# The scale of a state-space layer's gates taken on GpSimd: one power of minus one half in place of a root on ScalarE and a reciprocal on VectorE

## The chip, the cores and the metric

The kernel runs on one core of a Trainium2 chip. A core has five engines that each take their own instructions in order and meet only at semaphores: TensorE (PE, matmuls), VectorE (DVE), ScalarE (ACT), GpSimd (POOL) and SyncE (SP, which issues DMAs). The metric is the device time of one execution in microseconds.

## The reference

A block of three residual layers for 4 sequences of 128 tokens with 128 channels: a cross attention with 16 heads over 2048 keys, a gated linear recurrence (a state-space layer), and a two-layer perceptron with binary weights. The change lies in the second. Cut to it:

```python
u_scaled = exp(log_gamma) * einsum('btd,nd->btn', u, Win_n)
delta_raw, b_raw, c_raw = split(einsum('btd,kd->btk', u, Wp) + bp, 3)
delta = softplus(delta_raw + delta_bias)
a = minimum(exp(-delta * softplus(alpha_log)), 1.0 - 1e-4)
b, c = tanh(b_raw), tanh(c_raw)
p, r, q = a * a + c * c, b * b, a * b
disc = (p - r) * (p - r) + 4.0 * q * q
lam_max = 0.5 * (p + r + sqrt(disc + EPS))
scale = maximum(sqrt(lam_max + EPS), 1.0)
a, b, c = a / scale, b / scale, c / scale
# state z_t = a_t z_{t-1} + b_t u_scaled_t, by a scan over t
y = einsum('btn,on->bto', c * z_shifted, Wout_n)
```

## The kernel before

The attention comes first and takes most of the span: a loop over 128 units (4 sequences x 8 pairs of heads x 4 chunks of 512 keys). Behind it the rest of the block works on all 512 tokens, in two halves of 256 columns (`cols(h)`, two sequences each); channels lie on the 128 partitions. A half of a gate is a tile of 128x256 in fp32. All gates are named slices of one buffer, which the profile shows as `k_parts` since they reuse its memory; `q_r` in the profile is `q_r1`, and `q` is the tile of the scan's states (`STATE`).

Each engine's program is written out by hand, and its order is the order in which it works. For the gates it is:

- ScalarE does absolute value, exp, ln, tanh, squares and the root of the discriminant `G_D` (L1010, semaphore `disc_root`). Then it takes the root of `0.5 * G_L + EPS` for each half (L1013, `scale_ready`), touches Gelu so that its table is loaded (L1015), and goes on with the copies and the Gelus of the perceptron (L1021).
- VectorE adds `G_S + G_D` into `G_L` for both halves (L1488), clamps it from below at 2.0 (L1490, `lam_ready`), and multiplies U by the gain and B (`scale_input`, L1485). Then, for half 0: `invert(0)`, the reciprocal of `G_L` (L1504, `inv_ready`); `scale_gates(0)`, A and U times `G_INV` (L1509, L1511); `scan(0)` (L1518); `outputs(0)`, C times the state (L1499). Then `invert(1)`; the sum of y of half 0 with its layer norm's moments (L1521 to L1426); `scale_gates(1)`; the normalisation of half 0 (L1432); `scan(1)`; `outputs(1)`; and the same norm for half 1.
- GpSimd waits for `inv_ready` and multiplies C by `G_INV` for each half (L1164), and then takes the power of minus one half of the layer norm's variances (`root_inv_halves(1)`, L1035), two columns for each half. The exponent is the tile `neg_half`, filled with -0.5.
- TensorE projects the raw gates (L750 to L758), waits for `scale_ready` of half 0, and multiplies a tile of ones by itself 11 times (L352, fillers whose result nobody reads; the profile counts two matmuls for each). Then come y of half 0 (L733), 12 more fillers, the transposes of half 0 (L358), y of half 1, the hidden layer (L773) and the output layer (L782), the last two for half 0 and half 1 in turn.
- VectorE adds the result to the residual (L1541), and SyncE stores it.

Of the kernel before, what the change touches and what calls it, by code (L numbers as in the profile page):

```python
# [28 lines left out]
ALU = mybir.AluOpType  # L29
ACT = mybir.ActivationFunctionType  # L30
AX = mybir.AxisListType

P = 128
# [5 lines left out]
EPS = 1e-12  # L39
# [4 lines left out]
def perceiver_block(nc, x, ctx_in, mask, Wq, bq, Wk, bk, Wv, bv, Wo, bo, W_in, W_out, Wp, bp,  # L44
# [34 lines left out]
    with ctx:  # L79
        def sb(name, shape, dt=F32):  # L80
            return ctx.enter_context(nc.sbuf_tensor(name, shape, dt))
# [32 lines left out]
        neg_half = sb("neg_half", [P, B])  # L114
# [35 lines left out]
        sv = sb("sv", [P, 12])  # L150
# [57 lines left out]
        def once(name):  # L208
            return sems[name] if name in sems else sem(name)
# [6 lines left out]
        HALF = TOK // 2  # L216
# [8 lines left out]
        def cols(h):  # L225
            return slice(HALF * h, HALF * h + HALF)
# [120 lines left out]
        def _(pe):  # L347
# [389 lines left out]
            def finish():  # L737
                pe.wait_ge(o_ready, B)
                for h in range(2):
                    turn_half(h, o_nat, once("oN_turned"))  # L740
                for h in range(2):
                    pe.wait_ge(once("oNT_ready"), h + 1)
                    by_token(h, PROJ, xnT, wT[:, W_O, :], once("attn_done"))
                keep_busy(TURN, WARM_LN2)
                for h in range(2):
                    pe.wait_ge(once("ln_ready"), 2 * h + 2)
                    turn_half(h, xn, once("ln_turned"))
                for h in range(2):
                    pe.wait_ge(once("lnT_ready"), h + 1)
                    pe.matmul(bank(h, RAW_DELTA)[:, 0:HALF], wT[:, W_P, :], xnT[:, cols(h)], start=True, stop=True  # L750
                              ).then_inc(once("ssm_done"), 1)
                for h in range(2):
                    for i in range(2):
                        t = pe.matmul(bank(h, RAW_BC)[:, HALF * i:HALF * i + HALF], wT[:, W_P + 1 + i, :],
                                      xnT[:, cols(h)], start=True, stop=True)
                    t.then_inc(once("ssm_done"), 1)
                for h in range(2):
                    pe.matmul(bank(h, RAW_U)[:, 0:HALF], wT[:, W_IN, :], xnT[:, cols(h)], start=True, stop=True  # L758
                              ).then_inc(once("ssm_done"), 1)
                pe.wait_ge(once("scale_ready"), 1)  # L760
                keep_busy(TURN, WARM_Y)
                def project_y(h):
                    pe.wait_ge(once("yhat_ready"), h + 1)
                    by_token(h, Y, q_r1, wT[:, W_OUT, :], once("y_done"))

                def turn_mlp(h):
                    pe.wait_ge(once("ln_ready"), B + 2 * h + 2)
                    turn_half(h, xn, once("ln_turned"))

                def hidden(h):  # L770
                    pe.wait_ge(once("lnT_ready"), 2 + h + 1)
                    for i in range(HB):
                        t = pe.matmul(bank(h, HIDDEN + i // 2)[:, HALF * (i % 2):HALF * (i % 2) + HALF], w1T[:, i, :],  # L773
                                      xnT[:, cols(h)], start=True, stop=True)
                        if i % 2 == 1:
                            t.then_inc(once("h_done"), 1)

                def mlp_out(h, blocks):
                    for i in blocks:
                        pe.wait_ge(once("gelu_ready"), HB * h + i + 1)  # L780
                        for b in halves[h]:
                            t = pe.matmul(bank(h, OUT)[:, P * (b % 2):P * (b % 2) + P],  # L782
                                          probs[:, i, 0, P * b:P * b + P], w2T[:, i, :],
                                          start=(i == 0 and b % 2 == 0), stop=(i == HB - 1), skip_group_check=True)
                    return t

                project_y(0)
                keep_busy(4 + TURN, WARM_Y0)
                turn_mlp(0)
                project_y(1)  # L790
                hidden(0)
                mlp_out(0, range(0, 2))
                turn_mlp(1)
                mlp_out(0, range(2, HB)).then_inc(once("mlp_done"), 1)
                hidden(1)
                mlp_out(1, range(HB)).then_inc(once("mlp_done"), 1)
# [13 lines left out]
        def _(act):  # L810
# [197 lines left out]
            for h in range(2):  # L1008
                act.wait_ge(once("disc_ready"), h + 1)
                act.activation(G_D[:, cols(h)], G_D[:, cols(h)], ACT.Sqrt).then_inc(once("disc_root"), 1)  # L1010
            for h in range(2):
                act.wait_ge(once("lam_ready"), h + 1)
                act.activation(G_L[:, cols(h)], G_L[:, cols(h)], ACT.Sqrt, bias=sv[:, 9:10], scale=0.5  # L1013
                               ).then_inc(once("scale_ready"), 1)
            act.activation(sv[:, 8:9], ones[:, 0:1], ACT.Gelu)  # L1015
            for h in range(2):
                act.wait_ge(once("ln_turned"), 2 + h + 1)
# [8 lines left out]
        def _(gp):  # L1026
# [133 lines left out]
            root_inv_halves(0)  # L1160

            for h in range(2):
                gp.wait_ge(once("inv_ready"), h + 1)
                gp.tensor_tensor(G_CS[:, cols(h)], G_C[:, cols(h)], G_INV[:, cols(h)], ALU.mult  # L1164
                                 ).then_inc(once("c_scaled"), 1)
# [4 lines left out]
        def _(dve):  # L1170
# [268 lines left out]
            def each(s, op, *waits):  # L1439
                before_this = own_steps[0]  # L1440
                for h in range(2):
                    for name in waits:
                        if name == "own":
                            dve.wait_ge(once("own_step"), before_this - 1 + h)
                        else:
                            dve.wait_ge(once(name), h + 1)
                    op(h, cols(h)).then_inc(once("own_step" if s == "own" else s), 1)
                    if s == "own":
                        own_steps[0] += 1
# [33 lines left out]
            def scale_input(h):  # L1483
# [1 line left out]
                dve.scalar_tensor_tensor(U_S[:, cols(h)], bank(h, RAW_U)[:, 0:HALF], sv[:, 7:8], G_B[:, cols(h)],  # L1485
                                         ALU.mult, ALU.mult).then_inc(once("u_ready"), 1)

            each("own", lambda h, t: dve.tensor_tensor(G_L[:, t], G_S[:, t], G_D[:, t], ALU.add),  # L1488
                 "s_ready", "disc_root")
            each("lam_ready", lambda h, t: dve.tensor_scalar(G_L[:, t], G_L[:, t], 2.0, None, ALU.max), "own")  # L1490
            for h in range(2):
                scale_input(h)
            by_t = lambda a, h: a[:, cols(h)].rearrange("p (b t) -> p b t", t=T)
# [1 line left out]
            def outputs(h):  # L1495
# [2 lines left out]
                dve.wait_ge(once("first_step_ready"), 1)  # L1498
                dve.tensor_tensor(by_t(q_r1, h)[:, :, 1:T], by_t(G_CS, h)[:, :, 1:T], by_t(STATE, h)[:, :, 0:T - 1],  # L1499
                                  ALU.mult).then_inc(once("yhat_ready"), 1)  # L1500

            def invert(h):
                dve.wait_ge(once("scale_ready"), h + 1)
                dve.reciprocal(G_INV[:, cols(h)], G_L[:, cols(h)]).then_inc(once("inv_ready"), 1)  # L1504

            def scale_gates(h):
                t = cols(h)
# [5 lines left out]
            def scan(h):  # L1513
                dve.wait_ge(once("a_scaled"), h + 1)
                dve.wait_ge(once("u_scaled"), h + 1)
                for b in halves[h]:
# [3 lines left out]

            add_y = lambda h: dve.scalar_tensor_tensor(by_half(x_sb, h), bank(h, Y)[:, 0:HALF], norm_inv[:, 1:2],  # L1521
                                                       by_half(x_sb, h), ALU.mult, ALU.add)
            invert(0)
            scale_gates(0)
            scan(0)
            outputs(0)
            invert(1)
            add_and_moments(1, 0, add_y, "y_done")
            scale_gates(1)
            normalise_half(1, 0)  # L1530
# [50 lines left out]
```

## Time and profile before

| | |
|---|---|
| median of 3 runs | 290.27 us (286.96 to 290.95) |
| profiled execution | 289.0 us |
| its span, first to last instruction | 287.2 us |
| mean granted clock of TensorE | 0.97 of full |
| busy: TensorE, VectorE, ScalarE, GpSimd | 259.2, 223.5, 209.8, 100.8 us |
| instructions | 9806 |

All rows come from the one profiled execution. Its own time is 1.8 us above its span (launch and end). It lies 1.3 us under the median of the three runs.

### The profile page before, as it was taken

The page shows a single profiled execution, that of the slowest core. Times are in us where ns is not written, and L with a number is a line of the kernel's source. Part 1 is how long each engine was busy: PE and PEld are TensorE (multiplying, and loading weights), DVE is VectorE, ACT ScalarE, POOL GpSimd, SP SyncE. Part 2 cuts the span into 40 slices and gives each one's busy share as a digit, 9 for nine tenths or more (in the row PEclk, how much of TensorE's full clock was granted, in tenths as well). Part 3 has the DMA queues.
Part 4 walks back from the last instruction along what each step waited for, and adds up shares of the span by engine and source line. Part 5 has one row for each costly group of instructions (what it writes and reads, how often), then busy time and mean ns, then how long its engine had stood idle before and what let it go on. Part 6 is the DMA issues. An engine that isn't in the chain of part 4 may idle for free.

```text
span 287.2 us, 9806 instructions
## 1 busy us (share of the span) xinstructions
PE 259.2 (90%) x3981; PEld 187.0 (65%) x3981; DVE 223.5 (78%) x407; ACT 209.8 (73%) x441; POOL 100.8 (35%) x225
## 2 busy tenths in 40 slices
PE   7898689999999999999999999999999996750975
PEld 6485357676766676676777777777777664640955
DVE  5776888887877998878888888979888960529971
ACT  2675358888888878888888888888888787198232
POOL 6366775633344343333334454511111220100220
PEclk9999979999999999999999999999999999795799
DMA  6896944786432323242424332222222100000001
GB/s 200 294 316 174 286 120 140 229 235 192 159 123 80 119 68 121 66 129 79 135 74 135 93 105 66 67 67 66 66 88 76 34 3 5 1 0 0 0 0 41
DMA packets 21081, 30.55 MB, mean 106 GB/s; under 512 B 4272, under 2 KB 15052, under 8 KB 20908
## 3 DMA queue, kind: packets, MB, share of 16 engines
q1 hardware_dynamic: 17708, 28.00, 32.0%
q0 software_dynamic: 624, 1.06, 1.4%
q10 hardware_dynamic: 2704, 0.85, 1.3%
q8 instruction: 33, 0.54, 0.8%
q14 instruction: 12, 0.10, 0.1%
HBM read 22.43 MB, written 7.47 MB: 104 GB/s over the span
## 4 chain that ended last, share of the span: by engine, by line
PE 75%; DVE 10%; DMA 5%; ACT 4%; issue 4%; POOL 1%; ACTq 1%; SPq 0%; POOLq 0%; DVEq 0%
PE ps L504 24%; PE ps L487 14%; PE ps L463 11%; PE ps L597 5%; PE ps L515 4%; PE ps L358 4%; PE ps L558 4%; PE ps L550 4%; DMA w_kv<-in_L_xattn_Wq_dram 2%; DVE pmax L1315 2%; DMA k_rows<-k_parts_dram 1%; DMA k_parts_dram<-k_parts 1%; ACT probs L887 1%; DVE k_parts L1504 1%; PE ps L374 1%
## 5 line engine op out<-in xcount | busy, mean ns | idle before, releaser
L1315 DVE TENSOR_REDUCE pmax<-ps 128x2 f32<-128x1024 f32 x128 | 156.1, 1224 | 28.6 <-PE ps L463 27.9
L887 ACT ACTIVATE probs<-ps 128x512 f32<-128x512 f32 x256 | 138.8, 596 | 18.8 <-PE ps L487 16.5
L504 PE MATMUL ps<-probs,v_all 128*9 128x128 f32 x2048 | 80.5, 275 | 1.6 <-ACT probs L887 1.0
L463 PE MATMUL ps<-k_rows,q_all 56*128 56x512 bf16 x256 | 77.9, 384 | 3.0 <-DVE pmax L1315 2.2
L487 PE MATMUL ps<-q_max,k_rows 59*128 59x128 bf16 x1024 | 80.1, 218 | 0.2 <-DVE q_max L1327 0.2
L487 PEld LDWEIGHTS ps<-q_max,k_rows 59*128 59x128 bf16 x1024 | 54.3, 94 | 4.1 <-ACT probs L887 2.2
L504 PEld LDWEIGHTS ps<-probs,v_all 128*9 128x9 f32 x2048 | 43.3, 90 | 15.9 <-ACT probs L887 1.9
L1124 POOL CAST max_cols<-negmax 128x2 bf16<-128x2 f32 x32 | 6.1, 192 | 120.0 <-DVE negmax L1321 120.0
L463 PEld LDWEIGHTS ps<-k_rows,q_all 56*128 56x128 bf16 x256 | 23.2, 93 | 21.9 <-issue 11.3
L352 PE MATMUL ps<-ones 128*128 128x128 f32 x76 | 12.7, 338 | 11.0 <-ACT k_parts L1013 10.1
L352 PEld LDWEIGHTS ps<-ones 128*128 128x128 f32 x76 | 12.1, 252 | 11.4 <-ACT k_parts L1013 10.5
L820 ACT ACTIVATE v_all<-ps 128x256 f32<-128x256 f32 (+1 forms) x24 | 10.9, 456 | 9.0 <-PE ps L374 5.0
L597 PE MATMUL ps<-power 128*128 128x128 f32 x96 | 17.1, 300 | 0.0
L597 PEld LDWEIGHTS ps<-power 128*128 128x128 f32 x96 | 12.5, 190 | 5.2 <-issue 3.9
L515 PEld LDWEIGHTS ps<-gather,oT_sb 128*128 128x128 f32 x64 | 9.5, 188 | 7.6 <-issue 7.3
L1072 POOL TENSOR_TENSOR k_r<-k,k_parts 128x512 f32<-128x512 f32 x12 | 14.1, 1174 | 1.0
L1078 POOL TENSOR_TENSOR k_parts<-k_r,k_parts 128x512 bf16<-128x512 f32 x12 | 13.9, 1162 | 1.0
L820 ACT ACTIVATE ctxT<-ps 128x512 f32<-128x512 f32 x16 | 9.5, 595 | 6.1 <-PE ps L358 6.0
L515 PE MATMUL ps<-gather,oT_sb 128*128 128x18 f32 x64 | 12.7, 274 | 0.5 <-ACT oT_sb L820 0.5
L820 ACT ACTIVATE xnT<-ps 128x256 f32<-128x256 f32 (+2 forms) x6 | 2.3, 383 | 14.0 <-PE ps L358 14.0
L550 PE MATMUL ps<-ctxT,kvT 128*128 128x256 f32 x32 | 11.2, 431 | 1.2 <-DVE q_max L1327 1.2
L358 PE MATMUL ps<-ident,ctx_buf 128*128 128x128 f32 x64 | 11.0, 299 | 1.0 <-DMA ctx_buf<-in_ctx_dram 1.0
(186 smaller groups left out, 329.3 us busy)
## 6 DMA issues: line engine op xcount, KB each, us to landing
k_rows<-k_parts_dram SPq DMA_DIRECT2D x59, 192.0 KB
k_parts_dram<-k_parts SPq DMA_DIRECT2D x16, 384.0 KB, 3.9
ctx_buf<-in_ctx_dram SPq DMA_DIRECT2D x16, 256.0 KB, 6.1
k_rows<-k_parts_dram SPq DMA_DIRECT2D x59, 32.0 KB
mask_sb<-in_mask_1x1xSxS_ff_dram SPq DMA_DIRECT2D x1, 1024.0 KB, 8.6
q_all<-q_rows_dram SPq DMA_DIRECT2D x2, 336.0 KB
k_rows<-k_parts_dram POOLq DMA_DIRECT2D x3, 192.0 KB, 4.0
q_rows_dram<-q_parts SPq DMA_DIRECT2D x2, 288.0 KB, 3.9
```

Of the source, the lines that this page charges most:

```text
L352: pe.matmul(ps[:, bank, 0:P], ones[:, :], ones[:, :], start=True, stop=True)
L358: return pe.transpose(dst, src, ident[:, :])
L463: return pe.matmul(ps[:, bank + h, :], q_all[rows, i % PAIRS, i // PAIRS, :], k_rows[rows, i % 4, 512 * c:512 * c + 512], start=not masked ...
L487: t = pe.matmul(dst, k_rows[rows, i % 4, at:at + P], q_max[rows, i % 2, :], start=not masked, stop=True, skip_group_check=masked)
L504: t = pe.matmul(ps[at:at + HEAD_COLS, 6, 0:P], v_all[:, KT * (i // PAIRS) + 4 * c + j, first + HEAD_COLS * h: first + HEAD_COLS * h + HEAD ...
L515: return pe.matmul(ps[:, 7, 384:384 + 2 * HEAD_COLS], oT_sb[:, i % 2, :], gather[:, :], start=True, stop=True)
L550: pe.matmul(ps[:, 7, half], kvT[:, 0, :], ctxT[:, n % EARLY, half], start=True, stop=True).then_inc(k_done, 1)
L597: t = pe.matmul(ps[:, 7, P * w:P * w + P], power[:, k % 2, w, :], power[:, k % 2, w, :], start=True, stop=True)
L820: act.activation(dst, src, ACT.Copy).then_inc(s, n)
L887: act.activation(probs[:, u % CHUNKS, h, :], ps[:, key_bank(u, h), :], ACT.Exp).then_inc(probs_ready, 1)
L1072: gp.tensor_tensor(r1, k_all, k_parts[:, 0, keys], ALU.subtract).then_inc(split_k_step, 1)
L1315: dve.tensor_reduce(pmax[:, i % 2, :, c], ps[:, bank:bank + 2, :], AX.X, ALU.max).then_inc(pmax_ready, 1)
```

## The change

ScalarE's second pair of roots and VectorE's pair of reciprocals are gone. The sum on VectorE takes 2 EPS with it, and the clamp multiplies by 0.5, so that `G_L` now holds the square of the scale. GpSimd raises that tile of 128x256 to the power -0.5, one half of the tokens at a time, ahead of its multiplication of C; the exponent is one column of `neg_half` read for all 256. TensorE's fillers wait for both clamps in place of the first root.

```diff
--- before.py
+++ after.py
@@ -757,7 +757,7 @@
                 for h in range(2):
                     pe.matmul(bank(h, RAW_U)[:, 0:HALF], wT[:, W_IN, :], xnT[:, cols(h)], start=True, stop=True
                               ).then_inc(once("ssm_done"), 1)
-                pe.wait_ge(once("scale_ready"), 1)
+                pe.wait_ge(once("lam_ready"), 2)
                 keep_busy(TURN, WARM_Y)
                 def project_y(h):
                     pe.wait_ge(once("yhat_ready"), h + 1)
@@ -1008,10 +1008,6 @@
             for h in range(2):
                 act.wait_ge(once("disc_ready"), h + 1)
                 act.activation(G_D[:, cols(h)], G_D[:, cols(h)], ACT.Sqrt).then_inc(once("disc_root"), 1)
-            for h in range(2):
-                act.wait_ge(once("lam_ready"), h + 1)
-                act.activation(G_L[:, cols(h)], G_L[:, cols(h)], ACT.Sqrt, bias=sv[:, 9:10], scale=0.5
-                               ).then_inc(once("scale_ready"), 1)
             act.activation(sv[:, 8:9], ones[:, 0:1], ACT.Gelu)
             for h in range(2):
                 act.wait_ge(once("ln_turned"), 2 + h + 1)
@@ -1160,6 +1156,9 @@
             root_inv_halves(0)
 
             for h in range(2):
+                gp.wait_ge(once("lam_ready"), h + 1)
+                gp.tensor_tensor(G_INV[:, cols(h)], G_L[:, cols(h)], neg_half[:, 0:1].broadcast_to((P, HALF)), ALU.pow
+                                 ).then_inc(once("inv_ready"), 1)
                 gp.wait_ge(once("inv_ready"), h + 1)
                 gp.tensor_tensor(G_CS[:, cols(h)], G_C[:, cols(h)], G_INV[:, cols(h)], ALU.mult
                                  ).then_inc(once("c_scaled"), 1)
@@ -1485,9 +1484,9 @@
                 dve.scalar_tensor_tensor(U_S[:, cols(h)], bank(h, RAW_U)[:, 0:HALF], sv[:, 7:8], G_B[:, cols(h)],
                                          ALU.mult, ALU.mult).then_inc(once("u_ready"), 1)
 
-            each("own", lambda h, t: dve.tensor_tensor(G_L[:, t], G_S[:, t], G_D[:, t], ALU.add),
+            each("own", lambda h, t: dve.scalar_tensor_tensor(G_L[:, t], G_D[:, t], 2.0 * EPS, G_S[:, t], ALU.add, ALU.add),
                  "s_ready", "disc_root")
-            each("lam_ready", lambda h, t: dve.tensor_scalar(G_L[:, t], G_L[:, t], 2.0, None, ALU.max), "own")
+            each("lam_ready", lambda h, t: dve.tensor_scalar(G_L[:, t], G_L[:, t], 2.0, 0.5, ALU.max, ALU.mult), "own")
             for h in range(2):
                 scale_input(h)
             by_t = lambda a, h: a[:, cols(h)].rearrange("p (b t) -> p b t", t=T)
@@ -1498,10 +1497,6 @@
                 dve.wait_ge(once("first_step_ready"), 1)
                 dve.tensor_tensor(by_t(q_r1, h)[:, :, 1:T], by_t(G_CS, h)[:, :, 1:T], by_t(STATE, h)[:, :, 0:T - 1],
                                   ALU.mult).then_inc(once("yhat_ready"), 1)
-
-            def invert(h):
-                dve.wait_ge(once("scale_ready"), h + 1)
-                dve.reciprocal(G_INV[:, cols(h)], G_L[:, cols(h)]).then_inc(once("inv_ready"), 1)
 
             def scale_gates(h):
                 t = cols(h)
@@ -1520,11 +1515,9 @@
 
             add_y = lambda h: dve.scalar_tensor_tensor(by_half(x_sb, h), bank(h, Y)[:, 0:HALF], norm_inv[:, 1:2],
                                                        by_half(x_sb, h), ALU.mult, ALU.add)
-            invert(0)
             scale_gates(0)
             scan(0)
             outputs(0)
-            invert(1)
             add_and_moments(1, 0, add_y, "y_done")
             scale_gates(1)
             normalise_half(1, 0)
```

## Rows read from the trace of the kernel before

**Rows 1.** The page: busy shares, and the chain that ended last

```profile
PE 259.2 (90%) x3981; PEld 187.0 (65%) x3981; DVE 223.5 (78%) x407; ACT 209.8 (73%) x441; POOL 100.8 (35%) x225
...
PE 75%; DVE 10%; DMA 5%; ACT 4%; issue 4%; POOL 1%; ACTq 1%; SPq 0%; POOLq 0%; DVEq 0%
...
PE ps L504 24%; PE ps L487 14%; PE ps L463 11%; PE ps L597 5%; PE ps L515 4%; PE ps L358 4%; PE ps L558 4%; PE ps L550 4%; DMA w_kv<-in_L_xattn_Wq_dram 2%; DVE pmax L1315 2%; DMA k_rows<-k_parts_dram 1%; DMA k_parts_dram<-k_parts 1%; ACT probs L887 1%; DVE k_parts L1504 1%; PE ps L374 1%
```

**Rows 2.** The chain that ended last, 265 to 288 us: start, duration, what

```profile
265.77 1.67 DVE k_parts L1504
...
270.06 1.66 DVE k_parts L1504
```

**Rows 3.** Timeline, 264 to 285 us: start, duration, instruction, [idle before]

```profile
264.50 0.48 DVE L1490 TENSOR_SCALAR k_parts<-k_parts 128x256 f32<-128x256 f32 x2
...
264.82 0.91 ACT L1013 ACTIVATE k_parts<-k_parts,sv 128x256 f32<-128x256 f32 x2 [1.10 <-DVE k_parts L1490]
...
265.38 4.22 PE L352 MATMUL ps<-ones 128*128 128x128 f32 x22 [10.05 <-ACT k_parts L1013]
...
267.47 0.43 DVE L1509 TENSOR_TENSOR k_parts<-k_parts 128x256 f32<-128x256 f32 x1
...
267.51 0.97 POOL L1164 TENSOR_TENSOR k_parts<-k_parts 128x256 f32<-128x256 f32 x1 [17.08 <-DVE k_parts L1504]
...
267.81 0.95 DVE L1511 TENSOR_TENSOR k_parts<-k_parts 128x256 f32<-128x256 f32 x1
...
271.80 0.73 POOL L1164 TENSOR_TENSOR k_parts<-k_parts 128x256 f32<-128x256 f32 x1 [3.32 <-DVE k_parts L1504]
...
272.87 0.17 DVE L1426 TENSOR_SCALAR var_eps<-mv 128x2 f32<-128x2 f32 x1
...
273.11 0.80 POOL L1035 TENSOR_TENSOR rstd<-var_eps,neg_half 128x2 f32<-128x2 f32 x1 [0.58 <-DVE var_eps L1426]
...
273.95 0.60 DVE L1432 TENSOR_SCALAR xn<-x_sb,mv,rstd 128x128 f32<-128x128 f32 x2 [0.26 <-POOL rstd L1035]
...
274.61 0.44 PE L358 MATMUL ps<-ident,xn 128*128 128x128 f32 x2 [1.10 <-DVE xn L1432]
...
277.33 1.70 ACT L1021 ACTIVATE probs<-ps,vec 128x256 f32<-128x256 f32 x4 [1.86 <-PE ps L773]
...
278.03 0.69 POOL L1035 TENSOR_TENSOR rstd<-var_eps,neg_half 128x2 f32<-128x2 f32 x1 [4.12 <-DVE var_eps L1426]
...
282.32 1.95 PE L782 MATMUL ps<-w2T,probs 128*128 128x128 f32 x16
```

**Rows 4.** GpSimd's instructions grouped by line and shape: busy, mean ns, idle

```profile
L1126 POOL TENSOR_TENSOR nm_r<-negmax,max_cols 128x2 f32<-128x2 f32 x32 | 6.3, 196 | 2.6
...
L1035 POOL TENSOR_TENSOR rstd<-var_eps,neg_half 128x2 f32<-128x2 f32 x4 | 2.9, 729 | 17.5 <-DVE var_eps L1426 17.5
...
L1156 POOL TENSOR_TENSOR x_bo<-x_sb,bo_rows 128x128 f32<-128x128 f32 x4 | 1.8, 454 | 0.0
...
L1164 POOL TENSOR_TENSOR k_parts<-k_parts 128x256 f32<-128x256 f32 x2 | 1.7, 849 | 20.4 <-DVE k_parts L1504 20.4
...
L1052 POOL TENSOR_TENSOR rstd<-var_eps,neg_half 128x3 f32<-128x3 f32 x1 | 0.9, 877 | 0.6 <-DVE var_eps L1181 0.6
...
L1159 POOL TENSOR_TENSOR norm_inv<-norm_inv,neg_half 128x2 f32<-128x2 f32 x1 | 0.7, 714 | 0.0
...
L1048 POOL TENSOR_TENSOR rstd<-var_eps,neg_half 128x1 f32<-128x1 f32 x1 | 0.6, 563 | 2.8 <-DVE var_eps L1181 2.8
```

**Rows 5.** TensorE by stretch: length, busy (matmuls), granted clock, DMA share, GB/s

```profile
258.00:260.00 2.00, 0.00 (x0) 0.58 0.00 0
...
266.00:268.00 2.00, 2.00 (x11) 0.50 0.00 0
...
268.00:270.00 2.00, 1.60 (x12) 0.86 0.00 0
...
274.60:284.30 9.70, 8.62 (x56) 1.00 0.05 15
```

## Prediction

> **What bounds the kernel now.** I read the page first: TensorE is busy 90% of the span and holds 75% of the chain that ended last, but GpSimd only 35% [rows 1]. Those shares describe the attention loop, whose three matmul lines (L504, L487, L463) alone are 49% of the chain. The change lies in the gates after it, so I read the timeline of that stretch. Up to about 274 us it is a chain of small steps on VectorE and ScalarE, and TensorE only turns filler matmuls. The three steps to look at are the two reciprocals of 128x256, which stand on VectorE and on the chain with 1.67 and 1.66 us [rows 2], and the root ahead of them on ScalarE, 0.91 us for two halves, of which the first lies between the clamp and the first reciprocal [rows 3]. GpSimd is idle for 17.08 us before its first multiply there [rows 3]. The idleness is real; what the new work costs on that engine is the question, and the view that groups GpSimd's instructions by shape answers it.
>
> **What the power costs.** The kernel already takes powers of minus one half on GpSimd, on tiny tiles: 563 ns for one column of 128 partitions (x1), 714 ns and a mean of 729 ns for two (x1 and x4), 877 ns for three (x1) [rows 4]. The step from one to two columns is 151 ns, from two to three 163 ns, and from one to three 314/2 = 157 ns each. That is a price by the column, above a fixed 563 - 157 = 406 ns. The ordinary operations are in the same view for scale: a subtraction takes 196 ns for two columns, an addition 454 ns for 128, a multiplication 849 ns on average for 256 [rows 4]; from 2 to 128 columns that is (454 - 196)/126 = 2.0 ns a column, and from there to 256 3.1 ns or, by the undisturbed one of 0.73 us [rows 3], 2.1 ns. So an ordinary operation's price by the column is the same for short and for long rows, and the power's is some 75 times as high. The change asks for 256 columns, twice. By the line through the three sizes one costs 0.41 + 256 x 0.157 = 40.6 us.
>
> No row shows a power of more than three columns, so I bound it. Below stands the ordinary operation on the same tile, 0.73 us [rows 3]. Above, the steepest pair of single readings, 563 ns and the 0.80 us of one two-column power [rows 3, 4], gives 237 ns a column and 61 us. I take 40.6 us, since the three sizes lie on one line within 6 ns a column and the ordinary operations show that such a line holds on this engine; the shallowest pair, 563 ns and the 0.69 us of another two-column power [rows 3, 4], gives 0.127 us a column and some 33 us. The exponent is now one column read 256 times in place of a tile of its own; I cost that at nothing, since 256 exponents had to be delivered either way.
>
> Two rules of the Trainium skill speak the other way. The page GPSIMD Engine Reference, section 3.1 (Elementwise: side-by-side cycle accounting), gives some 2.6 cycles an element for a two-input operation; read as a rule for all of them, an estimate by it is 0.56 us and a fixed part for this tile. The trace agrees for the multiplication and not for the power. Its section 7 (Performance pitfalls for Q7 kernels) says that a dependent chain of fp32 steps goes faster when unrolled into at least four independent ones. No row here shows whether the power's code does so for long rows.
>
> **Part by part.** The addition on VectorE becomes one with a second addend, and the clamp gets a multiplication by 0.5. I leave the additions as they are and the clamps of both halves at 0.48 us from 264.50 on [rows 3], with a few hundredths for an error. Cost nothing: it is the same number of passes over the same tile. The first root waited for the first clamp and began at 264.82 [rows 3]; less 0.04 us for the handover the clamp ends at 264.78.
>
> Removed from ScalarE: the two roots, 0.91 us [rows 3]. Behind them is only the load of the table for the activation of the hidden layer, which comes up to 0.9 us earlier and is not needed before the first such activation at 277.33 [rows 3]. Removed from VectorE: the two reciprocals [rows 2].
>
> Added on GpSimd: two powers, each ahead of the multiplication that it already did. The engine takes its instructions in order, so the queue is power 0, C x INV of half 0, power 1, C x INV of half 1, and then the two-column power for the layer norm of half 0. What is queued there behind power 1 is needed by VectorE for that normalisation; and VectorE itself waits in order at the scaling of A of half 0, with the scan, the outputs, the sum of y and all of the second half queued behind it. The scaling of U needs INV as well, so nothing of the scan can begin.
>
> The new sequence, with a wait of 0.07 us for each handover (the variance ends at 272.87 + 0.17 = 273.04, and the power that waits for it begins at 273.11 [rows 3]):
> - power 0 begins at 264.78 + 0.07 = 264.85 and ends at 305.45;
> - C x INV of half 0, with the longer of its two durations, 0.97 us [rows 3]: 305.45 + 0.07 + 0.97 = 306.49;
> - power 1 has waited for nothing (both clamps are long done): it ends at 306.49 + 40.6 = 347.09;
> - C x INV of half 1: 348.13; the layer norm's power of 0.80 us: 348.93; VectorE's normalisation begins 0.04 us later, at 348.97.
> Before, that normalisation began at 273.95 [rows 3]. From it on the order of work is the old one, to the end. The scalings of half 1 run on VectorE from 347.14 and, with the first half's 0.43 and 0.95 us [rows 3], end at 348.5 and stay hidden. First half: gates at 305.5, y at about 308 (the outputs were ready at 270.06, when the second reciprocal began, 2.6 us after the first ended [rows 2]); all of its work fits under power 1, with over 30 us to spare. The shift is 348.97 - 273.95 = 75.0 us. With C for one power it is 2C - 6.2 us; the 6.2 is what was between clamp and normalisation before and is not done any more or is overlapped.
>
> **TensorE's clock.** The wait that starts the eleven filler matmuls moves from the first root to the second clamp, so the 4.22 us of them (from 265.38 today) begin some 0.3 us earlier and end near 269, almost 40 us before y of half 0 [rows 3]. The granted clock falls in a stretch without matmuls, to a mean of 0.58 in 258 to 260, and is 0.50 (1.2 GHz) while the fillers begin. They ran at 0.50 in 266 to 268, and the mean of 0.86 in 268 to 270 puts the return to full (2.4 GHz) at 268.6, 3.2 us after the first of them [rows 5]. Today the tail is all at 2.4 GHz: 1.00 in 274.6 to 284.3 [rows 5]. After the change the matmuls of y of half 0 and the fillers behind it are hidden under power 1, and then TensorE has nothing until 349 us. The tail starts at 1.2 GHz. Its matmuls are nearly one chain, from the transposes at 274.61 to the last line's 1.95 us from 282.32 [rows 3]: TensorE is busy for 8.6 of those 9.7 us [rows 5]. If some 3 to 4 us of it run at half speed before the clock is back, they do 1.5 to 2 us less work: I add 2.0 us. The bounds are nothing (the fillers' clock survives) and 8.6 us (it never rises in the tail).
>
> **The sum.** 75.0 + 2.0 = +77.0 us. The profiled execution took 289.0 us, 287.2 of them the span; the span would be 364.2 and the time 366.0. The median of the three runs, 290.27, is 1.3 us above the profiled one and they spread over 4 us; on the median it is 367.3, and I say 367.
>
> **Rivals.**
> 1. The power overlaps its columns once there are many of them, as it can't with three. At a quarter of 157 ns a column C = 0.41 + 10.0 = 10.4 us, the shift 2 x 10.4 - 6.2 = 14.6, with the clock 16.6: 307 us. For it: only sizes 1 to 3 are seen. (The section 7 of the Trainium skill's page above describes such a gain.) Against it: neither two nor three columns are cheaper than a line. Chance 0.12.
> 2. The power costs what an ordinary operation on the tile does, C = 0.73, and what the small ones show is a fixed cost that grows for another reason. (It is what section 3.1 of that page of the Trainium skill would have.) Then INV of half 0 is there at 265.6 and VectorE goes on when its multiplication of U by the gain and B is done and the reciprocal would begin, at 265.77, in place of 265.77 + 1.67 = 267.44 [rows 2]: 1.7 us won; the second reciprocal (1.66 us on the chain) covered the way of y through TensorE, 0.9 us of which stays as a wait, so 0.8 more. 2.5 us faster, 288 us. By 2C - 6.2 + 2.0 the change wins as long as C stays under 2.1 us, 7 ns a column. Against it: two columns alone take 0.7 us where an ordinary one takes 0.2. Chance 0.03.
> 3. The line, but the clock stays at 1.2 GHz through the tail: 367 + 6.6 = 374 us. Against it: the fillers brought it up in some 3 us. Chance 0.09.
> 4. Dearer than the line, 61 us each: 2 x 61 - 6.2 + 2 = +118, 408 us, should long rows or other values (before, the power saw variances; now numbers from one upwards) cost more. Chance 0.04.
>
> **How the numbers follow.** Forecast 0.72, rivals 0.12, 0.03, 0.09 and 0.04. What a measurement of this kernel can tell from no change is about 2%, 5.8 us. No case reaches 5.8 us of gain, since the best is 2.5; I leave 0.01. Within 2% needs 2C - 6.2 + 2.0 < 5.8, C under 5.0 us or 18 ns a column: rival 2 and the cheap end of rival 1, 0.04 in all. Slower: 0.95. The range: by the line 151 to 163 ns a column are 364 to 370 us; the shallowest pair is 352; rival 3 reaches 374, and a little on both sides for the spread of the runs: 345 to 380, which leaves out rivals 1, 2 and 4, 0.19.
>
> **What would show it.** Right: two powers on GpSimd of about 40 us each, GpSimd's busy time at some 180 us, VectorE waiting for them twice, for almost 40 and then for some 36 us; a granted clock of 0.50 at the start of the tail; C x INV still under 1 us. The attention loop before 244 us is the same. Wrong: powers of 10 us or less; or the second half's power overlapped by something that I hold to be queued behind it.

## The result, and the profile after

The changed kernel takes 366.81 us (median of 4 runs, 365.78 to 367.89) against 290.03 us (4 runs): 1.267 times as long, 95% interval 1.257 to 1.277. The forecast was 367. Here and below, ratios and their intervals leave out executions in a slower state that some runs show, so they differ slightly from the quotient of the medians. The profiled execution has a span of 364.9 us, 77.7 more than before.

The page of the changed kernel, with its busy times, the granted clock in 40 slices and the chain by engine, answers to [rows 1]:

```profile
PE 263.0 (72%) x3981; PEld 190.3 (52%) x3981; DVE 220.9 (61%) x405; ACT 209.1 (57%) x439; POOL 183.8 (50%) x227
...
PEclk9999899999999999999999999989665555855559
...
PE 63%; POOL 24%; DVE 6%; ACT 3%; issue 2%; DMA 1%; ACTq 0%; DVEq 0%; POOLq 0%
```

TensorE's busy time is the same to within 4 us, VectorE and ScalarE have a little less, and GpSimd has 83 us more, which it did not have on the chain before and now has: 24% of the chain against 1%. The clock row shows where the time lies, in the last quarter of the span, with TensorE at half clock for most of it. The first 244 us hold the same 233.3 us of matmuls in both kernels.

The timeline of the changed kernel from the clamp to the last addition answers to [rows 3] (lines have moved: the clamp is L1489, the power L1160, C x INV L1163, the scalings L1504 and L1506, the layer norm's power L1031, the normalisation L1431):

```profile
264.36 0.49 DVE L1489 TENSOR_SCALAR k_parts<-k_parts 128x256 f32<-128x256 f32 x2
...
264.73 41.13 POOL L1160 TENSOR_TENSOR k_parts<-k_parts,neg_half 128x256 f32<-128x256 f32 x1 [14.44 <-DVE k_parts L1489]
...
305.89 0.43 DVE L1504 TENSOR_TENSOR k_parts<-k_parts 128x256 f32<-128x256 f32 x1 [40.25 <-POOL k_parts L1160]
...
306.23 0.95 DVE L1506 TENSOR_TENSOR k_parts<-k_parts 128x256 f32<-128x256 f32 x1
...
306.86 41.29 POOL L1160 TENSOR_TENSOR k_parts<-k_parts,neg_half 128x256 f32<-128x256 f32 x1
...
348.19 0.43 DVE L1504 TENSOR_TENSOR k_parts<-k_parts 128x256 f32<-128x256 f32 x1 [36.68 <-POOL k_parts L1160]
...
349.16 0.87 POOL L1031 TENSOR_TENSOR rstd<-var_eps,neg_half 128x2 f32<-128x2 f32 x1
...
350.07 0.60 DVE L1431 TENSOR_SCALAR xn<-x_sb,mv,rstd 128x128 f32<-128x128 f32 x2 [0.59 <-POOL rstd L1031]
...
352.85 3.62 PE L773 MATMUL ps<-xnT,w1T 128*128 128x256 f32 x8
...
362.14 0.42 DVE L1534 TENSOR_TENSOR xn<-ps,x_bo 128x256 f32<-128x256 f32 x1 [2.99 <-PE ps L782]
```

Read it as one queue. The power of half 0 begins 0.08 us after its clamp, which ends at 264.65, and lasts 41.13 us; VectorE has been idle for 40.25 us when its first scaling begins, just after the power's end. Half 0's scalings, scan, y and the moments of its layer norm are done under the second power, 41.29 us, after which VectorE has been idle for 36.68 us. From the clamp's start to the normalisation's start it is 350.07 - 264.36 = 85.7 us; before it was 273.95 - 264.50 = 9.45 [rows 3]. That is 76.3 us of the 77.7. The rest is behind it: from the normalisation to the last addition 362.14 - 350.07 = 12.07 us. In the kernel before the same addition began at 284.31, so that it was 10.36: 1.7 us more.

TensorE's windows in that tail answer to [rows 5] (length, busy time with its number of matmuls, granted clock, DMA share, GB/s):

```profile
350.00:352.00 2.00, 0.85 (x3) 0.50 0.00 0
...
352.00:354.00 2.00, 2.00 (x7) 0.50 0.00 0
...
354.00:356.00 2.00, 2.00 (x6) 0.50 0.00 0
...
356.00:358.00 2.00, 2.00 (x17) 0.85 0.00 0
```

The tail begins at 0.50 (1.2 GHz) and the clock is back during 356 to 358. The hidden layer of half 0 takes 3.62 us at the low clock; that of half 1, at the high one, 1.89. Eight executions with a power in them and TensorE idle for over 6 us ahead of the tail were profiled; from the normalisation to the last addition they took 11.71 to 12.51 us.

### The profile page after: what moved, and what is told of

It reads as the page before. It is cut to its first block, busy times and chain, and to the rows that moved or that the text cites. A ratio compares the mean times of both kernels' runs of the same rounds, so it can differ in the third digit from the quotient of the medians.

```text
span 364.9 us, 9804 instructions
## 1 busy us (share of the span) xinstructions
PE 263.0 (72%) x3981; PEld 190.3 (52%) x3981; DVE 220.9 (61%) x405; ACT 209.1 (57%) x439; POOL 183.8 (50%) x227
## 4 chain that ended last, share of the span: by engine, by line
PE 63%; POOL 24%; DVE 6%; ACT 3%; issue 2%; DMA 1%; ACTq 0%; DVEq 0%; POOLq 0%
POOL k_parts L1160 23%; PE ps L504 19%; PE ps L487 11%; PE ps L463 9%; PE ps L597 4%; PE ps L358 3%; PE ps L515 3%; PE ps L558 3%; PE ps L550 3%; PE ps L374 2%; PE ps L369 2%; PE ps L773 1%; DMA x_sb<-in_x_dram 1%; DVE pmax L1314 1%; PE ps L782 1%
## 5 line engine op out<-in xcount | busy, mean ns | idle before, releaser
L1160 POOL TENSOR_TENSOR k_parts<-k_parts,neg_half 128x256 f32<-128x256 f32 x2 | 82.4, 41211 | 14.4 <-DVE k_parts L1489 14.4
L1504 DVE TENSOR_TENSOR k_parts<-k_parts 128x256 f32<-128x256 f32 x2 | 0.9, 426 | 76.9 <-POOL k_parts L1160 76.9
L358 PE MATMUL ps<-ident,xn 128*128 128x128 f32 x16 | 3.9, 346 | 39.4 <-DVE xn L1431 38.2
L733 PE MATMUL ps<-wT,q_r 128*128 128x128 f32 x8 | 2.4, 461 | 40.2 <-DVE q_r L1498 40.2
L358 PEld LDWEIGHTS ps<-ident,xn 128*128 128x128 f32 x16 | 2.2, 168 | 40.3 <-DVE xn L1431 38.8
L733 PEld LDWEIGHTS ps<-wT,q_r 128*128 128x128 f32 x8 | 1.9, 321 | 40.8 <-DVE q_r L1498 40.8
L352 PE MATMUL ps<-ones 128*128 128x128 f32 x76 | 13.5, 353 | 10.7 <-DVE k_parts L1489 9.7
L352 PEld LDWEIGHTS ps<-ones 128*128 128x128 f32 x76 | 13.0, 268 | 11.1 <-DVE k_parts L1489 10.1
```

The costliest lines, as they stand in the source:

```text
L352: pe.matmul(ps[:, bank, 0:P], ones[:, :], ones[:, :], start=True, stop=True)
L358: return pe.transpose(dst, src, ident[:, :])
L1160: gp.tensor_tensor(G_INV[:, cols(h)], G_L[:, cols(h)], neg_half[:, 0:1].broadcast_to((P, HALF)), ALU.pow).then_inc(once("inv_ready"), 1)
```

## Experiments

**Is it a price by the column? (e1)** Each power is cut into pieces; nothing else changes.

```diff
-gp.tensor_tensor(G_INV[:, cols(h)], G_L[:, cols(h)], neg_half[:, 0:1].broadcast_to((P, HALF)), ALU.pow
-                 ).then_inc(once("inv_ready"), 1)
+at = HALF * h
+for n in ((16, 48, 64, 128), (4, 8, 32, 84, 128))[h]:
+    ...
+    gp.tensor_tensor(G_INV[:, at:at + n], G_L[:, at:at + n], neg_half[:, 0:1].broadcast_to((P, n)), ALU.pow
+                     ).then_inc(once("inv_ready" if last else "piece"), 1)
+    at += n
```

> Each power is cut into pieces of 16, 48, 64 and 128 columns (half 0) and of 4, 8, 32, 84 and 128 (half 1), the same columns in all. Price by the column (my theory): a piece of n columns takes 0.41 + 0.159 n us, so 1.0, 1.7, 5.5, 8.0, 10.6, 13.8 and 20.8 us for 4, 8, 32, 48, 64, 84 and 128 columns, and the kernel is some 3 us longer than the changed one for the seven added fixed parts, 370 us. Rival (short rows cost more by the column than long ones): the line bends between 3 columns and 256, and the sum of the pieces is well above 85 us.

370.11 us, one run. The groups of GpSimd by shape, in this kernel (busy, mean ns of one, idle before):

```profile
L1165 POOL TENSOR_TENSOR k_parts<-k_parts,neg_half 128x128 f32<-128x128 f32 x2 | 41.4, 20720 | 0.2
...
L1165 POOL TENSOR_TENSOR k_parts<-k_parts,neg_half 128x64 f32<-128x64 f32 x1 | 10.5, 10512 | 0.0
...
L1165 POOL TENSOR_TENSOR k_parts<-k_parts,neg_half 128x32 f32<-128x32 f32 x1 | 5.4, 5407 | 0.0
...
L1165 POOL TENSOR_TENSOR k_parts<-k_parts,neg_half 128x16 f32<-128x16 f32 x1 | 2.9, 2893 | 14.5 <-DVE k_parts L1495 14.5
...
L1165 POOL TENSOR_TENSOR k_parts<-k_parts,neg_half 128x8 f32<-128x8 f32 x1 | 1.6, 1627 | 0.0
...
L1165 POOL TENSOR_TENSOR k_parts<-k_parts,neg_half 128x4 f32<-128x4 f32 x1 | 1.2, 1184 | 0.0
```

The pieces of 48 and 84 columns took 7.99 and 13.73 us. From 8 to 16 columns it is 158 ns a column, from 16 to 128 (20720 - 2893)/112 = 159, and from 128 to the changed kernel's 256, 41.2 us on average, 160. The line does not bend. Only the piece of 4 columns is off it, with 1.18 us where the line has 1.04. The pieces of half 0 span 42.14 us and those of half 1 42.66, 84.8 together and not well above 85, so the rival is out.

**Does the kernel lose anything but the powers' own time? (e2)** The operation of the two instructions becomes a multiplication, so that the scale is not computed; the rest is the changed kernel.

```diff
-neg_half[:, 0:1].broadcast_to((P, HALF)), ALU.pow
+neg_half[:, 0:1].broadcast_to((P, HALF)), ALU.mult
```

> The operation of the two big instructions on GpSimd is a multiplication in place of the power, so the scale is wrong and the rest of the work the same; everything else is as in the changed kernel. My theory (all of the loss is the power's price by the column): 0.73 to 0.97 us for each, 2.5 us faster than the kernel before, 287.5 us, and the tail at full clock. Rival (GpSimd in this place costs more than its own time, by handovers and by instructions that run in order behind it): slower than the kernel before, by 1 us or more.

287.43 us (10 runs) against 289.39 for the kernel before beside it (13 runs), a ratio of 0.9955, interval 0.9915 to 0.9996. So the powers are all of the loss. With a multiplication in their place (the output is then wrong) the kernel takes what the kernel before takes or slightly less: the difference is under 1% and barely clear of the noise. Its timeline:

```profile
262.76 0.50 DVE L1489 TENSOR_SCALAR k_parts<-k_parts 128x256 f32<-128x256 f32 x2
...
263.13 0.61 POOL L1160 TENSOR_TENSOR k_parts<-k_parts,neg_half 128x256 f32<-128x256 f32 x1 [14.44 <-DVE k_parts L1489]
...
263.31 5.07 PE L352 MATMUL ps<-ones 128*128 128x128 f32 x22 [9.72 <-DVE k_parts L1489]
...
266.80 0.42 DVE L1498 TENSOR_TENSOR q_r<-k_parts,q 128x254 f32<-128x254 f32 x1
...
268.17 1.06 PE L733 MATMUL ps<-wT,q_r 128*128 128x128 f32 x4
...
269.27 0.48 DVE L1516 SCALAR_TENSOR_TENSOR x_sb<-ps,norm_inv,x_sb 128x256 f32<-128x256 f32 x1 [2.04 <-PE ps L733]
...
282.03 0.42 DVE L1534 TENSOR_TENSOR xn<-ps,x_bo 128x256 f32<-128x256 f32 x1 [2.99 <-PE ps L782]
```

From the clamp to the last addition it is 282.03 - 262.76 = 19.27 us against 284.31 - 264.50 = 19.81 before: 0.5 us won inside the stretch, where I had said 2.5. (The clamp also began 1.7 us earlier, at 262.76, which is no gain of the change: the first transpose behind the attention began between 243.0 and 246.3 us in the executions profiled here.) The outputs of half 0 end at 267.22, but y begins at 268.17 behind the fillers, which start after 9.72 us without a matmul, at half clock, and take 5.07 us. VectorE then waits 2.04 us for y, as its row shows. How long the fillers hold y differs between executions: the same 22 matmuls took 4.11 us in the changed kernel's profile, 4.46 in f1's and 5.07 here.

**Fewer fillers in its way (g3).** The same with 8 fillers ahead of y of half 0 and 15 behind.

```diff
-WARM_LN2, WARM_Y, WARM_Y0 = 8, 11, 12
+WARM_LN2, WARM_Y, WARM_Y0 = 8, 8, 15
```

> e2 (a multiplication in place of the power) with 8 fillers ahead of y of half 0 and 15 behind it, in place of 11 and 12. In e2 y of half 0 stood behind the fillers: they ended at 268.4 while the scan's outputs were there at 267.2, and y ran at half clock. If that is what kept e2's gain from the clamp to the last addition at 0.5 us in place of 2.5: y begins when the outputs are ready and another 0.5 to 1 us is won, 286.8 us. Rival (the gain is lost elsewhere, since the layer norm behind y is itself no faster): no difference from e2.

```profile
263.54 0.48 DVE L1489 TENSOR_SCALAR k_parts<-k_parts 128x256 f32<-128x256 f32 x2
...
267.57 0.42 DVE L1498 TENSOR_TENSOR q_r<-k_parts,q 128x254 f32<-128x254 f32 x1
...
268.05 0.71 PE L733 MATMUL ps<-wT,q_r 128*128 128x128 f32 x4 [0.18 <-DVE q_r L1498]
```

The outputs end at 267.99 and y begins at 268.05. The last addition begins at 281.56, so the stretch is 18.02 us: 1.8 us shorter than before, and 1.2 shorter than with 11 fillers. So between these two traces the fillers were what held back 1.2 of the 2.0 us that were missing. The median does not show it: 287.59 us (12 runs), ratio 0.9956, interval 0.9921 to 0.9992, the same as with 11, where 286.8 was expected. A difference of 1.2 us is within what these runs spread by, and 11 fillers at 4.11 us would have held y for some 0.2 us only (an estimate from e2's row of the outputs, 267.22, and its first filler, 263.31). The step is shown in two traces and not in the time.

**Is it the repeated exponent column? (e3)** The exponents come from a tile of their own.

```diff
+neg_tile = sb("neg_tile", [P, 256])
+gp.memset(neg_tile[:, :], -0.5).then_inc(once("neg_tile_ready"), 1)
...
-neg_half[:, 0:1].broadcast_to((P, HALF)), ALU.pow
+neg_tile[:, :], ALU.pow
```

> The exponents come from a tile of 128x256 filled with -0.5 in place of one column read 256 times. My theory: 41.2 us for a power, as with the one column, 367 us. Rival (the repeated column is what is slow): a power of 20 us or less and a time under 330 us.

366.73 us, one run, and the first of its powers:

```profile
264.86 41.24 POOL L1163 TENSOR_TENSOR k_parts<-k_parts,neg_tile 128x256 f32<-128x256 f32 x1 [14.77 <-DVE k_parts L1492]
```

41.24 us: it is not the column.

**Is it the values? (e4)** Every base is 1.0, so that the scale is lost.

```diff
-dve.tensor_scalar(G_L[:, t], G_L[:, t], 2.0, 0.5, ALU.max, ALU.mult)
+dve.tensor_scalar(G_L[:, t], G_L[:, t], 0.0, 1.0, ALU.mult, ALU.add)
```

> The clamp is replaced by a multiplication by 0 and an addition of 1, so that every base is exactly 1.0 and the scale is lost; the powers are the same in shape. My theory (a fixed number of steps for every column): 41.2 us each, 367 us. Rival (the price depends on the values, for instance by steps repeated until they settle): a power shorter by a quarter or more, 347 us or less.

364.72 us, one run, with

```profile
262.81 41.13 POOL L1160 TENSOR_TENSOR k_parts<-k_parts,neg_half 128x256 f32<-128x256 f32 x1 [14.44 <-DVE k_parts L1489]
...
304.94 41.30 POOL L1160 TENSOR_TENSOR k_parts<-k_parts,neg_half 128x256 f32<-128x256 f32 x1
```

The durations are those of the changed kernel within 0.01 us; the 2 us in the time are the start, 262.81 in place of 264.73. The price does not depend on these values. The clamp keeps every base of the changed kernel at 1.0 or above, so what is compared is such numbers with exactly 1.0; other bases on long rows were not tried.

**By the column or by the element? (f1)** Half 0's power in two instructions of 64 partitions.

```diff
+for k in range(1 if h else 2):
+    rows_ = slice(0, P) if h else slice(64 * k, 64 * k + 64)
...
-    gp.tensor_tensor(G_INV[:, cols(h)], G_L[:, cols(h)], ...
+    gp.tensor_tensor(G_INV[rows_, cols(h)], G_L[rows_, cols(h)], ...
```

> The power of half 0 is taken as two instructions of 64 partitions x 256 columns, one after the other; half 1 as in the changed kernel. My theory (a price by the column, whatever the number of partitions): 41.2 us for each of the two, and the kernel 41 us longer than the changed one, 408 us. Rival (a price by the element, so that 64 partitions cost half): 20.6 us each, 367 us.

409.22 us, one run, and in the groups of GpSimd:

```profile
L1165 POOL TENSOR_TENSOR k_parts<-k_parts,neg_half 64x256 f32<-64x256 f32 x2 | 82.2, 41118 | 14.5 <-DVE k_parts L1494 14.4
...
L1165 POOL TENSOR_TENSOR k_parts<-k_parts,neg_half 128x256 f32<-128x256 f32 x1 | 41.3, 41308 | 0.0
```

64 partitions cost what 128 do. The Trainium skill's page GPSIMD Engine Reference, section 2 (Architecture), says that each of eight cores works on its own 16 partitions, 16 lanes wide. If so, fewer partitions leave lanes idle and save no step, and the trace agrees, with 41.12 and 41.31 us.

**One half alone (f2).** Half 0 by root and reciprocal, half 1 by the power.

```diff
-for h in range(2):
+for h in range(1):
     act.wait_ge(once("lam_ready"), h + 1)
     act.activation(G_L[:, cols(h)], G_L[:, cols(h)], ACT.Sqrt, bias=sv[:, 9:10], scale=0.5
...
 for h in range(2):
+    if h == 1:
+        gp.wait_ge(once("lam_ready"), 2)
+        gp.tensor_tensor(G_INV[:, cols(1)], G_L[:, cols(1)], neg_half[:, 0:1].broadcast_to((P, HALF)), ALU.pow
+                         ).then_inc(once("inv_ready"), 1)
     gp.wait_ge(once("inv_ready"), h + 1)
...
-each("lam_ready", lambda h, t: dve.tensor_scalar(G_L[:, t], G_L[:, t], 2.0, None, ALU.max), "own")
+each("lam_ready", lambda h, t: dve.tensor_scalar(G_L[:, t], G_L[:, t], 2.0, 0.5 if h else None, ALU.max, *((ALU.mult,) if h else ())), "own")
...
-invert(1)
```

> Half 0 has its root and reciprocal as in the kernel before; only half 1 is taken by a power on GpSimd, which stands there behind the multiplication of C of half 0. My theory: GpSimd is free at 268.5, the power ends at 309.7, C x INV and the layer norm's power follow, and VectorE's normalisation begins at 311.6 in place of 273.95: 37.7 us, and 1.7 for the tail at half clock, 329.5 us. Rival (half 0's power, being the first on the path, holds most of the loss, and that of half 1 is partly covered by half 0's work): under 310 us.

328.03 us (4 runs), ratio 1.132, interval 1.126 to 1.139: 38 us longer than the kernel before.

```profile
263.17 0.49 DVE L1494 TENSOR_SCALAR k_parts<-k_parts 128x256 f32<-128x256 f32 x2
...
267.11 41.31 POOL L1165 TENSOR_TENSOR k_parts<-k_parts,neg_half 128x256 f32<-128x256 f32 x1
...
310.33 0.60 DVE L1436 TENSOR_SCALAR xn<-x_sb,mv,rstd 128x128 f32<-128x128 f32 x2 [0.59 <-POOL rstd L1035]
...
322.81 0.42 DVE L1544 TENSOR_TENSOR xn<-ps,x_bo 128x256 f32<-128x256 f32 x1 [2.99 <-PE ps L782]
```

From the clamp to the normalisation it is 47.2 us, 37.7 more than before, as expected; the tail is 12.48. Half 1's power alone costs half of the loss, although half 0's work up to the moments of its layer norm goes on under it, since that work ends under 5 us after the power begins (at 271.68, against 267.11). The rival is out.

**The clock in the tail (f3, g1, g2).** 150 fillers in place of 12 behind y of half 0, then 174, the latter beside the changed kernel once more.

```diff
-WARM_LN2, WARM_Y, WARM_Y0 = 8, 11, 12
+WARM_LN2, WARM_Y, WARM_Y0 = 8, 11, 150
```

> 150 filler matmuls in place of 12 behind y of half 0, so that TensorE works until shortly before the tail begins, under the second power. My theory (the tail's 1.7 us more are the granted clock): the tail runs at 2.4 GHz from its first matmul and the kernel takes 1.7 us less than the changed one, 365.1 us. Rival (the tail is longer for another reason, such as the order in which the two halves arrive): 366.8 us, with the clock up.

367.62 us (4 runs). It did not do what it was for: the fillers end at 344.17, TensorE is idle for 6.39 us, and the tail starts at the low clock again. Windows and one line of the timeline:

```profile
320.00:340.00 20.00, 20.00 (x182) 1.00 0.00 1
...
340.00:350.00 10.00, 4.17 (x38) 0.95 0.00 0
...
350.00:352.00 2.00, 1.03 (x3) 0.50 0.00 0
```

```profile
350.56 0.69 PE L358 MATMUL ps<-ident,xn 128*128 128x128 f32 x2 [6.39 <-DVE xn L1431]
```

> As f3, with 174 fillers in place of 150: at 0.22 us each at full clock they end near 349.5, about 1 us before the tail's first transpose, where 150 left TensorE idle for 6.39 us and the clock back at 0.50. Theory (the tail's additional time is the clock): the tail at 1.00 from its first matmul, 10.4 us from the normalisation's start to the last addition as in the kernel before instead of 12.1, and 1.7 us less than the changed kernel beside it. Rival (the two halves' order or the handovers): 12.1 us at full clock too.

> The changed kernel once more, as the measure for the run beside it: 366.8 us.

366.32 us (8 runs) for 174 fillers, 367.54 us (6 runs) for the changed kernel beside it. The ratios to the kernel before, 1.265 (1.260 to 1.269) and 1.268 (1.262 to 1.274), overlap, so the 1.2 us between them are not settled by the times. The 174's timeline and windows:

```profile
352.63 0.60 DVE L1431 TENSOR_SCALAR xn<-x_sb,mv,rstd 128x128 f32<-128x128 f32 x2 [0.59 <-POOL rstd L1031]
...
353.29 0.44 PE L358 MATMUL ps<-ident,xn 128*128 128x128 f32 x2 [0.97 <-DVE xn L1431]
...
354.39 0.71 PE L733 MATMUL ps<-wT,q_r 128*128 128x128 f32 x4 [0.67 <-DVE q_r L1498]
...
354.94 3.26 PE L773 MATMUL ps<-xnT,w1T 128*128 128x256 f32 x8
...
364.06 0.42 DVE L1534 TENSOR_TENSOR xn<-ps,x_bo 128x256 f32<-128x256 f32 x1 [2.99 <-PE ps L782]
```

```profile
350.00:352.00 2.00, 2.00 (x20) 1.00 0.00 0
...
352.00:354.00 2.00, 0.75 (x5) 1.00 0.00 0
...
354.00:356.00 2.00, 1.61 (x8) 0.83 0.00 0
...
356.00:358.00 2.00, 2.00 (x7) 0.50 0.00 0
```

This tail starts at 1.00, and its transposes and y have the durations of the kernel before, 0.44 and 0.71 us. Then the clock falls to 0.50 in the middle of the hidden layer, which takes 3.26 us, while TensorE is busy 1.61 of 2 us. The tail is 11.43 us, against 12.51 in the changed kernel profiled beside it (351.10 to 363.61), 12.07 in its first profile and 10.36 before. It is 0.3 us under the shortest of the eight tails that start at the low clock, 11.71 (e3). So half of the theory holds: up to the start of the hidden layer, 2.31 us behind the normalisation in both, this tail has the times of the kernel before, and the 1.1 us by which it is longer come with the low clock behind it. But keeping TensorE busy up to the tail did not keep the clock for the tail. Why it fell there stays open.

**A version without GpSimd (f4).** On the kernel before, the inverse as exp(-0.5 ln x) on ScalarE.

```diff
-    act.activation(G_L[:, cols(h)], G_L[:, cols(h)], ACT.Sqrt, bias=sv[:, 9:10], scale=0.5
+    act.activation(G_L[:, cols(h)], G_L[:, cols(h)], ACT.Ln, bias=sv[:, 9:10], scale=0.5
                    ).then_inc(once("scale_ready"), 1)
+for h in range(2):
+    act.wait_ge(once("scale_ready"), h + 1)
+    act.activation(G_INV[:, cols(h)], G_L[:, cols(h)], ACT.Exp, scale=-0.5).then_inc(once("inv_ready"), 1)
...
-invert(0)
...
-invert(1)
```

> On the kernel before: the scale's inverse as exp(-0.5 ln(x)) on ScalarE, with no reciprocal on VectorE and no power on GpSimd. It adds two table loads of 1.28 us. My theory: the load for the logarithm hides beside VectorE's addition and clamp, both logarithms end at 265.8, the load for the exponential at 267.1, and the first half is ready at 267.5, as before (267.44); the second reciprocal is gone from VectorE, of which 0.8 us were not covered: 0.8 us faster, 289.3 us. Rival (the table loads stand on the path with more than that): 1 us slower or more.

288.87 us (12 runs) against 290.03 (17 runs), ratio 0.9958, interval 0.9914 to 1.0003: no difference that the measurement can tell.

```profile
264.58 0.49 DVE L1494 TENSOR_SCALAR k_parts<-k_parts 128x256 f32<-128x256 f32 x2
...
267.77 0.43 DVE L1509 TENSOR_TENSOR k_parts<-k_parts 128x256 f32<-128x256 f32 x1 [1.92 <-ACT k_parts L1017]
...
267.81 1.83 POOL L1168 TENSOR_TENSOR k_parts<-k_parts 128x256 f32<-128x256 f32 x2 [17.31 <-ACT k_parts L1017]
...
269.16 1.08 DVE L1518 TENSOR_TENSOR_SCAN q<-k_parts 128x128 f32<-128x128 f32 x2
...
273.91 0.60 DVE L1436 TENSOR_SCALAR xn<-x_sb,mv,rstd 128x128 f32<-128x128 f32 x2 [0.26 <-POOL rstd L1039]
```

The first half is ready at about 267.7, where 267.5 was expected. From the clamp to the normalisation it is 9.33 us against 9.45 before: 0.1 us of the expected 0.8. Both halves' INV now come close together, so GpSimd does both its multiplications from 267.81 to 269.64, beside VectorE's scaling of U and the scan. The scan takes 1.08 us where it took 0.74 before. Measured from the clamp, the outputs are ready 0.55 us later: 0.2 because the scalings begin later and 0.3 by the scan. So most of what the missing reciprocal gave is gone.

## Why the prediction was right, step by step

**The power's price.** Forecast 40.6 us, from three tiles of 1 to 3 columns; measured 41.13 and 41.29. The slope was 157 ns a column by [rows 4] and is 159 to 160 on long rows. The two together are 82.4 us against 81.2: the 1.2 us missing from the sum are here. That the step to long rows was sound is shown by e1, that the exponent's form costs at most 0.1 us by e3, and that setting every base to 1.0 changes nothing by e4. The Trainium skill's page GPSIMD Engine Reference says in section 7 (Performance pitfalls for Q7 kernels) that a dependent chain of fp32 steps goes faster when unrolled into at least four; how the power's code is built no run shows, but no such gain appears in it, 159 ns a column up to 128 columns and 160 beyond. The same page of the Trainium skill gives 2.6 cycles an element for two inputs in section 3.1 (Elementwise: side-by-side cycle accounting), by the prediction's estimate 0.56 us and a fixed part for this tile. The multiplication in the power's place is near that, 0.61 and 0.79 us in e2; the measured power is 68 times the 0.61. Rivals 1 and 4 fell with the two durations of 41 us, and e1 shows why for rival 1: long rows are no cheaper by the column.

**The order on GpSimd and VectorE.** Forecast: power 0, multiplication, power 1, multiplication, layer norm's power, then the normalisation, 84.12 us from the start of power 0 (264.85 to 348.97). Measured 85.34 (264.73 to 350.07), and the difference is the powers' 1.2. VectorE waited 40.25 and 36.68 us, forecast almost 40 and some 36. f2 confirms that the two powers add up with no cover.

**The tail.** Forecast +2.0 us for the low clock, measured +1.7 in the profiled execution and 2.1 in that of the changed kernel's second profile (12.51 against 10.36). That the size came out is in part luck. The prediction had 3 to 4 us at the low clock; the mean of 0.85 in 356 to 358 puts the return at 356.6 (an estimate, worked out as the prediction did for 268.6), 5.9 us after the first transpose at 350.73. Up to the end of the first hidden layer that cost 2.2 us (6.40 us behind the normalisation against 4.20), and waits further on took up 0.5 of it, which the prediction had not counted. Rival 3, the whole tail at 1.2 GHz, did not come: the clock rose during 356 to 358.

**The sum.** 75.0 + 2.0 = 77.0 forecast. Measured, 76.26 + 1.71 - 0.14 (an earlier clamp) = 77.83, in the spans 77.7; the 0.1 between them lies behind the last addition. That the median came within 0.2 us of the forecast is closer than it could promise: the runs of the kernel before spread over 4 us, and the profiled execution lies 0.7 us above its own forecast of 366.0.

**What was off** is rival 2's price, which was not the forecast: 2.5 us faster for a power at an ordinary price. e2 won 0.5 in the trace and g3, with fewer fillers, 1.8. Two things were missed: the fillers, which start at half clock and last 5 us in e2, stand ahead of y in TensorE's order, and became the wait behind a shorter chain; and GpSimd's multiplications then fall beside VectorE's scalings and scan, of which the first scaling takes 0.87 us and the scan 1.08 in g3, against 0.43 and 0.74 before. The break-even given with rival 2, C under 2.1 us, is not borne out either. It uses 2C - 6.2, which counts GpSimd's queue alone and holds while that queue is what VectorE waits for. At e2's 0.61 and 0.79 us it would move the normalisation by -4.8 us; from the clamp to the normalisation e2 took 8.92 us against 9.45, a shift of -0.5. At what price the change stops paying was not measured.

## What to carry to other kernels

Read the price of an operation by its shape before moving it: two small instances of different width give a fixed part and a slope, and the slope decides. A power on GpSimd costs under 1 us for one to three columns (a row's norm) and 0.16 us for every further column, for 64 partitions as for 128; a root and a reciprocal of 128x256 together cost some 2.1 us (half of 0.91, and 1.67). An engine's idleness says nothing of what it would take for the work, and when a step gets shorter, what was sized to fill its time (here the fillers for the clock) becomes the next wait.

## What the runs showed of the hardware that was not expected

- The clock of TensorE fell to 0.50 during matmuls: in the kernel with 174 fillers it was 1.00 from 316 us to their end at 352.3 and on to 354, with a gap of 0.97 us and the lighter work of the transposes and y in it (TensorE busy 0.75 of 2 us); then it was 0.50 throughout 356 to 358 and came back in 358 to 360. In this execution a load kept up ahead of the stretch did not keep the clock through it.
- VectorE's scan of two 128x128 tiles took 0.73 us alone and 1.08 when it began beside a multiplication on GpSimd (e2, f4). Beside a power it depends on which: 0.74 us with e1's piece of 4 columns, 0.96 with the power of 256 columns, 1.07 when that one reads its exponents from a tile (e3). Why it differs was not looked into.
